# A new written-out order of work for the cross-attention of a three-layer decoder, with the input transposes moved in the DMA queue

## What is computed

```
x = layernorm(x + attention_1(x))                       # causal, with LoRA and output projection
h = x
x = ln1(h + self_attention(h))                          # 16 heads of 32
Q = split(x @ ca_wq + bq); K = split(ctx @ ca_wk + bk); V = split(ctx @ ca_wv + bv)
h = softmax(Q K^T / sqrt(32)) V                         # cross-attention, 224 queries, 750 keys
x = ln2(x + h)
x = ln3(x + relu(x @ fc1 + b1) @ fc2 + b2)              # then a layernorm
x = layernorm(x + bitlinear(gelu(bitlinear(x))))        # quantized feed forward
```

## Time and profile before

| | us |
|---|---|
| median of 3 runs | 3438.45 |
| lowest and highest of them | 3430.24 and 3458.22 |
| profiled execution, whole | 3440.53 |
| its span in the profile | 3438.7 |
| TensorE busy in the span | 3152.1 |
| VectorE busy in the span | 2621.7 |

### The profile page before, as it was taken

The page is one execution under the profiler, slowest core; times in us unless marked ns, Lnnn a source line. Parts: engine busy times, 40 slices in busy tenths (PEclk is TensorE's granted clock), DMA queues, the critical chain, the costliest instruction groups (busy, mean ns, idle before and its releaser), DMA issues.

```text
span 3438.7 us, 88599 instructions
## 1 busy us (share of the span) xinstructions
PE 3152.1 (92%) x35500; PEld 2441.7 (71%) x35500; DVE 2621.7 (76%) x4755; ACT 1999.4 (58%) x4522; POOL 1231.6 (36%) x1128
## 2 busy tenths in 40 slices
PE   6999999998999769999999999999979999999996
PEld 4987888887889647777777777777755556555562
DVE  5776788888889658888888888888855666666666
ACT  2665566566677536667677676766764434434342
POOL 0444521146665543334343344334122122131222
PEclk9999999999999889999999999999999999999998
DMA  3566555446554545445555545554352121121211
GB/s 98 174 185 214 180 163 154 135 123 199 164 158 136 158 115 132 118 118 134 131 123 128 132 120 118 125 128 109 86 188 58 44 53 44 41 59 44 53 38 46
DMA packets 445189, 405.71 MB, mean 118 GB/s; under 512 B 270471, under 2 KB 352523, under 8 KB 443630
## 3 DMA queue, kind: packets, MB, share of 16 engines
q1 hardware_dynamic: 444526, 399.78, 42.9%
q10 hardware_dynamic: 256, 0.26, 0.0%
HBM read 239.72 MB, written 109.52 MB: 102 GB/s over the span
## 4 chain that ended last, share of the span: by engine, by line
PE 58%; DMA 11%; DVE 10%; SPq 8%; ACT 5%; issue 4%; POOL 4%; ACTq 0%; POOLq 0%; DVEq 0%
PE at_ps L746 23%; PE at_ps L1394 8%; PE at_ps L890 5%; PE at_ps L870 5%; PE at_ps L833 4%; PE at_ps L1374 4%; DMA self_spill<-at_proj 3%; PE at_ps L1408 2%; DVE at_mx_cross L953 2%; DMA causal_spill<-at_proj 2%; DMA at_w_first<-cross_spill 2%; SPq L702 2%; PE at_ps L775 2%; DVE at_p L960 2%; ACT at_ps L913 1%
## 5 line engine op out<-in xcount | busy, mean ns | idle before, releaser
L960 DVE TENSOR_TENSOR at_p<-at_ps,at_p 125x448 f16<-125x448 f32 (+1 forms) x1280 | 781.0, 616 | 181.4 <-ACT at_ps L913 171.9
L912 ACT ACTIVATE at_p<-at_ps 125x448 f16<-125x448 f32 (+1 forms) x1280 | 698.3, 546 | 376.8 <-PE at_ps L870 355.5
L913 ACT ACTIVATE at_ps<-at_ps 125x448 f32<-125x448 f32 (+1 forms) x1280 | 699.7, 547 | 0.0
L953 DVE TENSOR_REDUCE at_mx_cross<-at_ps 128x1 f32<-128x750 f32 x512 | 476.0, 930 | 59.0 <-PE at_ps L833 57.8
L1033 POOL TENSOR_TENSOR at_o_sum<-at_o_raw 128x256 f32<-128x256 f32 x192 | 121.6, 633 | 918.2 <-ACT at_o_raw L919 918.0
L870 PE MATMUL at_ps<-at_stacks 97*112 97x224 f16 (+2 forms) x1792 | 338.9, 258 | 19.7 <-DMA at_stacks<-at_mrow 17.9
L1374 PE MATMUL at_ps<-at_xt,at_early 128*128 128x256 f16 x1792 | 307.0, 278 | 27.9 <-ACT at_w_first L1443 27.0
L890 PE MATMUL at_ps<-at_values,at_p 112*128 112x33 f16 (+3 forms) x7168 | 315.2, 185 | 13.5 <-ACT at_o_raw L919 7.5
L905 ACT ACTIVATE at_proj<-at_ps 128x448 f16<-128x448 f32 (+2 forms) x320 | 154.9, 484 | 271.8 <-PE at_ps L746 271.7
L956 DVE TENSOR_REDUCE at_mx<-at_ps 128x2 f32<-128x448 f32 x512 | 304.0, 610 | 8.4 <-PE at_ps L845 6.7
L890 PEld LDWEIGHTS at_ps<-at_values,at_p 112*128 112x128 f16 (+1 forms) x7168 | 284.0, 97 | 33.2 <-ACT at_o_raw L919 9.8
(11 more groups left out here) (202 smaller groups left out, 6761.7 us busy)
## 6 DMA issues: line engine op xcount, KB each, us to landing
at_x_res<-x SPq DMA_DIRECT2D x124, 256.0 KB, 2.9
cross_spill<-at_proj SPq DMA_DIRECT2D x64, 487.0 KB, 3.0
at_x_rows<-x SPq DMA_DIRECT2D x92, 256.0 KB, 4.4
at_prep<-bit SPq DMA_DIRECT2D x32, 512.0 KB, 4.6
at_early<-ctx SPq DMA_DIRECT2D x32, 512.0 KB, 4.1
at_stacks<-cross_spill SPq DMA_DIRECT2D x64, 243.5 KB, 3.6
causal_spill<-at_proj SPq DMA_DIRECT2D x64, 224.0 KB, 2.1
at_stacks<-causal_spill SPq DMA_DIRECT2D x128, 112.0 KB, 2.3
```

The lines of the kernel that those rows point to most:

```text
L912: act.activation(mem.p_hi[0:self.KC, n % 4, :], scores, ACT.Exp, scale=EXP_SCALE)
L913: act.activation(scores, scores, ACT.Exp, scale=EXP_SCALE).then_inc(self.exp_done, 1)
L953: dve.tensor_reduce(self.mx[:, at, t, h:h + 1], mem.ps_qk[:, :, 0:self.KT // 2], AX.XY, ALU.max).then_inc(self.max_done, 1)
L960: dve.tensor_tensor(mem.p_lo[0:self.KC, n % 4, :], mem.ps_st[0:self.KC, self.st_bank(b, g, n), 0:2 * T], mem.p_hi[0:self.KC, n % 4, :], AL ...
```

## The change

The four lines for the cross-attention are replaced. The tokens are the same, and each stands in the same line as before, except that c0 moves from the second line to the third, c2 and c3 from the third to the fourth, and c4 and c5 as told below. What each engine computes, the sizes and the number of instructions stay. c4 and c5 move from the fourth line to the first of the next batch, which the second part of the diff provides for: tokens of the inputs in the first line are now for the batch 1 ahead, not 2, and they are skipped in the first batch, whose successor's inputs are complete already.

```diff
-    "cross": (("E1 S2 V0 k0a M0 k0b M1 S3 q V1 M2 load row V2 S4 k1a M3 S5 k1b S6 residual V3 V4 M4 S7 S8 v0a S9 V5 "
-                 "M5 E0 v0b V6 S10 spill V7 V8 M6 S11 V9 S0 v1 splitx V10 M7 stack V11 S1",
-                 "splitc0 norm S2 E1 q k0a V0 V1 M0 S3 k0b M1 S4 k1a apply k1b S5 M2 V2 spill V3 V4 row S6 S7 v0a M3 "
-                 "S8 v0b V5 M4 E0 S9 loadc0 V6 S10 V7 V8 x0 M5 S11 v1 c0 V9 M6 S0 x1 V10 V11 M7 S1 stack",
-                 "splitc1 q E1 M0 S2 row S3 V0 V1 k0a M1 S4 k0b S5 k1a M2 V2 S6 k1b S7 V3 M3 loadc1 V4 S8 V5 S9 E0 c2 "
-                 "v0a spill M4 S10 V6 v0b M5 S11 V7 V8 c1 V9 c3 M6 S0 v1 S1 V10 V11 M7 stack",
-                 "E1 S2 q V0 V1 M0 S3 row S4 k0a M1 V2 k0b k1a M2 S5 k1b S6 M3 splitc2 V3 V4 S7 V5 E0 spill S8 v0a V6 "
-                 "M4 S9 stack S10 V7 v0b c4 M5 V8 S11 V9 V10 S0 M6 loadc2 S1 c5 v1 V11 M7 store"),
+    "cross": (("c4 S2 k0a M0 E1 k0b load V0 V1 residual M1 S3 q row M2 S4 S5 V2 k1a k1b M3 c5 S6 S7 V3 v0a V4 V5 E0 "
+                 "M4 S8 V6 S9 v0b S10 V7 M5 S11 spill stack V8 V9 splitx v1 M6 S0 V10 V11 S1 M7",
+                 "E1 x0 S2 q k0a M0 norm x1 S3 k0b V0 M1 S4 k1a splitc0 k1b V1 spill M2 S5 V2 apply V3 S6 M3 row S7 V4 "
+                 "V5 E0 S8 v0a M4 stack loadc0 S9 V6 V7 V8 M5 S10 v0b M6 S11 S0 V9 S1 v1 M7 V10 V11",
+                 "E1 splitc1 q S2 c0 k0a V0 c1 M0 S3 k0b row M1 S4 V1 V2 S5 V3 k1a M2 S6 k1b V4 spill V5 E0 M3 S7 S8 "
+                 "v0a V6 M4 S9 V7 S10 V8 M5 S11 v0b V9 V10 M6 S0 v1 V11 S1 stack loadc1 M7",
+                 "S2 k1a S3 k1b E1 q V0 M0 S4 spill k0a c2 M1 k0b c3 V1 M2 stack S5 V2 row S6 V3 V4 M3 S7 V5 S8 v0a M4 "
+                 "E0 S9 S10 V6 v0b store V7 M5 V8 S11 V9 V10 S0 M6 S1 v1 V11 M7 splitc2 loadc2"),
                (3, 2, 1, 2)),
...
                 elif token in layer.IN_JOBS:
-                    at, what = resolve(b + 2), (token, part)
+                    late = layer.cross and g == 0
+                    at, what = None if late and b == layer.b0 else resolve(b + (1 if late else 2)), (token, part)
```

## The result

| | before | after |
|---|---|---|
| median of 7 runs, same chip | 3444.41 us | 3472.31 us |
| profiled execution: span | 3438.7 us | 3456.0 us |
| batches 2 to 14, each | 80.34 us | 82.23 us |
| batch 15 | 77.5 us | 77.96 us |

A forecast was written before the change was run, and what follows sets the result against it. TensorE was taken to set the pace, idle 66 us for maxima and one stack. In 14 turns -2.84 + 0.4 + 2.9 + 1.4 = +1.86, +26 us, and +2 in the last two batches: 3466 us, range 3415 to 3492.

The forecast's parts named there:

- M6's cover: Fourth line: M6 would wait 0.8 us for its reduction, but S0's wait for the row covers it.
- What leaves: Third line's M0 no longer waits for the stack, nor loses clock there: -2.84 us a turn, moved transposes costing nothing.
- The row behind the stack: Fourth line: S0 waits for the row queued behind the stack, 2.9 us a turn, plus 1.4 for the clock.
- K: Fourth line: start of k0b, the last projection its spill waits for; row issued at K + 8.7, stack lands K + 12.3.
- The upper end: Fourth line: the row lands with the stack at K + 12.3, so S0 waits 2.9 us, not 1.3.
- the first rival: Fourth line: row passes the stack, lands 2.0 us behind its issue, S0 waits 1.3, clock stays up: 3424; chance 0.2.
- The clock: TensorE's clock falls to its lower level behind S0's wait in nearly every turn: +1.4 us.
- The slow rival: Fourth line: S0's wait passes 3 us (3.4), clock down for two stretches of 3.5 us: +53 us, 3491; chance 0.15.
- The maxima: All four lines: TensorE's waits for reductions of maxima go from 4.25 to 4.65 us a batch, +0.4, bounds -1 and +1.5.
- apply (1.0): Second line: apply, between M2 and M3, taken to hold VectorE 1.0 us, within 11.3 us of work behind some 2.0 of waits.
- E0's wait: A wait of 0.35 us at E0, predicted to stand in the new first line, counted among the maxima's waits.
- The 0.15: Each TensorE wait was taken to cost about 0.15 us more than its shown idle time.

The follow-up runs named there:

- e3: Kernel before with its old four lines, only the transposes placed anew: 3398.57 us, ratio 0.9885 to before, batch 77.50 us.
- e1: Changed kernel with the fourth line's row issued ahead of the stack in SyncE's queue: 3411.74 us, ratio 0.9915 to before, batch 78.48 us.
- e4: New lines with the row ahead of the stack, but transposes where they were before: 3443.75 us, ratio 1.0007 to before, batch 80.09 us.
- e2: Changed kernel with the fourth line's c2 and c3 behind the row, the row still behind the stack: 3451.16 us, ratio 1.0022 to before.
- e7: Changed kernel with a store and the context's 476 KB load put between stack and row in the fourth line: 3511.94 us, ratio 1.0188 to before.
- e11: Changed kernel with the fourth line's row issued from ScalarE's queue instead of SyncE's: 3426.57 us, ratio 0.9941 to before, batch 79.58 us.
- e5: e1 with norm at the second line's start and apply between the split and k1b: 3442.86 us, ratio 0.9970 to before, batch 80.74 us.
- e13: Changed kernel with GpSimd's split at the second line's start, row still behind the stack: 3451.77 us, ratio 1.0009 to before, batch 81.53 us.
- e9: e1 with GpSimd's split moved to the second line's start: 3398.13 us, ratio 0.9865 to before, batch 77.24 us.

## Why the prediction was right

| term, us a turn | predicted | measured | by |
|---|---|---|---|
| stack's wait and clock leave | -2.84 | -2.84 | e3: 77.50, before 80.34 |
| maxima, M6 not covered | +1.2 | +0.98 | e1, e3 (+0.9 without e1's one batch with a low clock) |
| row behind the stack, with clock, less M6's cover | +3.5 | +3.75 | after, e1 |
| sum | +1.86 | +1.89 | after, before |

**What leaves** was right to the hundredth, and so was the idea that batch 15 prices it. e4 shows that it needs the move of the transposes; that the moves themselves cost nothing is shown by e3. The price holds for the old lines: in the new ones, with M0 standing later, the same move is worth 1.6 (e1 against e4).

**The row behind the stack** was right in place, size and chain. On average K to spill is 2.25 (predicted 2.31), spill to the stack's landing 10.2 (10.0), S0 is ready at K + 9.45 (9.4), and its wait is 2.78 shown (predicted 2.9). The upper end, the landing with the stack, was the right choice, and the first rival is out: the row lands 3.78 behind its issue, not 2.0. The reason holds too, that the row can't pass what is ahead in its queue: it lands 0.1 to 0.3 behind the last transfer ahead of it in all turns of e2 and e7. In the changed kernel it always lands behind the last piece but one, by 0.2 to 0.9, and between 0.2 behind the landing of the last piece and 1.1 ahead of it. What the reason lacked is that a transfer of the other queue is not passed either (e11).

**The clock** fell in 13 of 14 turns (predicted "nearly every turn"). Of the 3.75, the wait without M6's cover is about 2.2 by its shown length, so 1.6 is the clock, as a remainder; predicted 1.4. The slow rival's mechanism exists: two turns of after, four of e5, eight of e13 and all of e7 have the low clock for 6.8 us. But the length of the wait alone doesn't decide it. Of five waits of 3.3 to 3.5 us in after only two have it, and in e5, where the wait is 2.38 in every turn, four of 14. It is so in the turns in which the clock fell 0.5 us or more before TensorE started again; in after these were two. That they were not more was not foreseen, so the clock's share owes something to luck.

**The maxima** were near for a wrong reason. The second line's waits, 2.0 predicted, are 2.15 shown at four places. The step that failed is "apply (1.0)": it takes 2.16 in its new place, because the split now runs beside it. Without that, in e9, the new lines take 77.24, 0.3 less than the old ones, where I had them worse by 1.2. My count from delays and cover was too high elsewhere: the first line shows 0.62 in two waits where I had 1.55 in three, and E0's wait did not appear. Two errors of over 1 us cancelled, and that is luck. The 0.15 that I added to each shown wait is not borne out either: e1 has four more waits a batch than e3 and 0.9 to 1.0 more of shown wait, and its undisturbed batch is 0.9 longer.

**The last two batches:** I had the row in time in batch 15, with 1.2 more than before. S0 waited 0.81 there, but M6 was covered, so the batch grew by 0.46. **The sum** is 28 us by the medians and 25 by the batches of the two profiles, against 28 predicted. The size of the row's cost and of what leaves was foreseen; that the maxima came out near was chance.

## What to carry to other kernels

When work is moved in a written-out order, check each step against what now runs beside it on every other engine, not only against its own queue: the same VectorE instruction took 0.54 us alone and 1.70 beside GpSimd. Give a small transfer that something waits for its place ahead of the large ones of its queue; price it by its issue behind theirs and by their landing, not by its size. In this kernel it landed just behind them, from a second queue too. Do the halves of a change alone: here one half was worth -1.2% and the whole +0.9%.

## What the runs showed of the hardware

- A DMA of 1.8 KB lands 1.7 us behind its issue with nothing large ahead, in 2.6 behind two transposes (e1), in 3.8 to 4.0 behind the four DMAs of a stack (after, e2), and in 4.5 with 0.9 MB more ahead (e7). It lands 0.12 to 0.30 behind the last transfer ahead of it in e2 and e7. From another queue, issued 0.3 to 1.1 behind the stack's first DMA, it takes 3.2 to 5.1 (e11).
- A plain DMA takes SyncE mostly 0.3 to 0.65 us of issue, and size does not order them: 0.34 for the spill of 487 KB, 0.43 for 56 KB, 0.62 for the row of 1.8 KB (after). Single ones took longer, as the stack's second in after with 1.2. Four of them moved the row by 2.1 us on average (e7).
- VectorE's TENSOR_SCALAR on 128x512 float32 from and to SBUF ends 0.28 us behind the GpSimd instruction that was running as it started: 0.54 alone, 1.70 in after, 0.86 and 2.34 in e5. Reductions and differences that read PSUM were not touched.
- The granted clock fell to its lower level, 0.50, behind waits of TensorE of 1.7 to 2.7 us in 8 of 14 turns of before (it stayed up behind others of 1.1 to 2.0), behind 1.4 to 2.7 in 9 of 14 of e2, and at 2.0 to 3.5 in 13 of 14 of after. It also fell at the pair of short waits of M4 and M5 (1.08 and 0.45), once in after and in e1 and three times in e4. It stays there for 3.4 us where it fell at the end of the wait or behind it, and for 6.8 us where it fell 0.5 us or more before TensorE had work again (e7 in all turns, e13 in 8, e5 in 4, after in 2).
